# Moving every third injection of the two cross-scan layers to GpSimd, and the product du to VectorE

## The reference

```python
delta = softplus(dts + delta_bias)                    # (192, L)
h = exp(delta * A[d, n]) * h + (delta * u) * B[n, l]  # the recurrence along l
y += h * C[n, l]                                      # summed over n
```

## Time and profile before

| | before |
|---|---|
| median of 3 runs | 3813.66 us (3811.82 to 3817.78) |
| the profiled execution's own time | 3815.76 us |
| its span, first to last instruction | 3813.9 us |
| cross layer 0, first injection to last scan | 1406.3 us |
| cross layer 3, first injection to last scan | 1411.9 us |
| mean granted TensorE clock | 0.779 |

### The profile page before, as it was taken

How to read it: one execution, slowest core, us unless ns; L and a number is a source line. 1 busy time by engine, 2 the same in 40 slices (tenths; PEclk the granted TensorE clock), 3 DMA queues, 4 the chain that set the end, 5 groups by cost and what they waited for, 6 DMA issues and landing times. The chain is left out here.

```text
span 3813.9 us, 26717 instructions
## 1 busy us (share of the span) xinstructions
PE 2849.4 (75%) x6084; PEld 648.1 (17%) x6084; DVE 3266.3 (86%) x2104; ACT 2051.3 (54%) x2278; POOL 2350.1 (62%) x1004
## 2 busy tenths in 40 slices
PE   6778777877887788435667677688778887887887
PEld 2111111111111211111111121111111111111111
DVE  1899999999999998585988924999999999999993
ACT  3465555656565655314555425556565556656562
POOL 1677767777776776003656504677676767776773
PEclk9677787878788877767789777677887778788778
DMA  2555546463655554103443405365546555564742
GB/s 57 136 126 139 138 125 143 119 161 97 160 129 133 124 133 117 28 0 84 117 106 85 99 5 122 99 160 133 129 115 142 135 128 126 132 153 109 157 119 62
DMA packets 140377, 436.95 MB, mean 115 GB/s; under 512 B 33429, under 2 KB 34139, under 8 KB 139915
## 3 DMA queue, kind: packets, MB, share of 16 engines
q1 hardware_dynamic: 140234, 435.53, 47.4%
HBM read 307.50 MB, written 6.82 MB: 82 GB/s over the span
## 5 line engine op out<-in xcount | busy, mean ns | idle before, releaser
L841 POOL TENSOR_TENSOR L_read<-L_state,L_c_rows 128x1024 f32<-128x1024 f32 x768 | 1809.0, 2362 | 757.1 <-DVE L_state L931 467.3
L931 DVE TENSOR_TENSOR_SCAN L_state<-L_decay,L_b_ps 128x1024 f32<-128x1024 f32 x768 | 1756.0, 2286 | 29.4 <-DVE L_b_ps L916 2.1
L651 PE MATMUL L_y_ps<-L_read,L_fold 128*64 128x512 f32 x3072 | 1255.0, 913 | 394.8 <-POOL L_read L841 375.5
L916 DVE TENSOR_TENSOR L_b_ps<-L_du,L_b_ps 128x1024 f32<-128x1024 f32 x768 | 937.5, 1221 | 236.0 <-issue 146.4
L777 ACT ACTIVATE L_decay<-L_delta,L_a_neg 128x1024 f32<-128x1024 f32 x768 | 876.4, 1145 | 406.7 <-DVE L_state L931 405.7
L767 ACT COPY L_b_ps<-L_b_rows 128x1024 f32<-128x1024 f32 x256 | 260.1, 1016 | 340.6 <-DVE L_state L931 220.6
L651 PEld LDWEIGHTS L_y_ps<-L_read,L_fold 128*64 128x64 f32 x3072 | 188.0, 161 | 1356.5 <-POOL L_read L841 1017.6
L1461 POOL TENSOR_TENSOR L_read<-L_state,L_c_rows 128x1024 f32<-128x1024 f32 x96 | 237.3, 2477 | 184.3 <-PE L_y_ps L1257 109.5
L1567 DVE TENSOR_TENSOR_SCAN L_state<-L_decay,L_b_ps 128x1024 f32<-128x1024 f32 x96 | 219.5, 2286 | 3.3
L626 PE MATMUL L_side_ps<-L_dbl,L_w_dt 128*128 128x512 f32 x216 | 182.4, 940 | 50.3 <-DVE L_sq_b L902 26.9
L626 PE MATMUL L_side_ps<-g_cm,L_w_u 96*128 (+1 forms) x216 | 179.7, 921 | 41.7 <-ACT L_u L695 40.0
(11 more groups left out here) (315 smaller groups left out, 2677.3 us busy)
## 6 DMA issues: line engine op xcount, KB each, us to landing
L_c_rows<-L_bc_dram SPq DMA_DIRECT2D x580, 256.0 KB, 4.0
L_b_rows<-L_bc_dram SPq DMA_DIRECT2D x580, 256.0 KB, 4.2
...
```

What stands on the lines that cost most here:

```text
L651: m = nc.tensor.matmul(y_ps[i * BLK:(i + 1) * BLK, c, :], fold[:, :], y_half(t, o, i), start=first, stop=last, skip_group_check=True)
L841: nc.gpsimd.tensor_tensor(read[:, t % READS, :], state[:, t % STATES, :], c_rows[:, g % 2, :], ALU.mult).then_inc(multiplied, 1)
L916: nc.vector.tensor_tensor(to[:, :], du2[:, d * NBLK + c, :], row[:, :], ALU.mult).then_inc(injected, 1)
L931: nc.vector.tensor_tensor_scan(state[:, t % STATES, way], decay[:, t % DECAYS, way], fed[:, way], 0.0, ALU.mult, ALU.add).then_inc(scanned, 1)
```

## The change

It does four things, in the cross-scan layers only. (1) The injection of c = 2 is done by POOL (`inject_c`, L850 in the changed file), from du2 and the SBUF copy of the row B, straight into the state buffer that the scan then reads and overwrites. It stands on POOL ahead of the product with C of c = 0 of its group, and waits for POOL's own last product of the group before, which read that state buffer. `b_rows` gets two buffers for it. (2) The decay of c = 2 goes to a PSUM tile, `work_ps`. This same tile holds the injection of c = 0, so ACT may write the decay of c = 2 only when the scan of c = 0 of that group is done; before, it needed only the scan three tiles back. (3) There is one PSUM tile for the row, `row_ps`; the injection of c = 1 is in place over it. So `copy_b` of the next group still waits for the scan of c = 1, and has only the scan of c = 2 beside it. (4) In the turns du is formed by DVE from the sum in `side_ps`, in two halves of 128 x 512 per block (L929), at tile `at` + 3; ACT's copy of the same half to delta waits for it (`sp_du`). At the heads of the layers POOL still forms du.

```diff
-        b_rows = sb("b_rows", [128, L])
+        b_rows = sb("b_rows", [128, 2, L])
-        b_ps = [ctx.enter_context(nc.psum_tensor(f"{name}_b_ps{i}", [128, L], F32)) for i in range(2)]
+        row_ps = ctx.enter_context(nc.psum_tensor(f"{name}_row_ps", [128, L], F32))
+        work_ps = ctx.enter_context(nc.psum_tensor(f"{name}_work_ps", [128, L], F32))
...
                 sp.wait_ge(b_ready, G + 1)
+                sp.wait_ge(injected_c, G + 1)
...
                 elif kind == "sum":
+                    if not isinstance(turn, Head):
+                        act.wait_ge(sp_du, 2 * (turn.next * NJ + j) + i + 1 - NJ)
                     ins = nc.scalar.copy(delta[:, j, s], side_ps[:, :])
+                    if i == 1:
+                        ins.then_inc(delta_ready, 1)
...
-                    nc.scalar.activation(decay[:, t % DECAYS, :], delta2[:, d * NBLK + c, :], ACT.Exp,
+                    g = t // NBLK
+                    if c == 2:
+
+                        act.wait_ge(scanned, number * NT + t - 1 + SCAN0)
+                    to = work_ps if c == 2 else decay[:, c, :]
+                    nc.scalar.activation(to[:, :], delta2[:, d * NBLK + c, :], ACT.Exp,
...
+            def inject_c(number, g):
+
+                d, last = g // NP, NBLK - 1
+                if g % NP == 0:
+                    pool.wait_ge(du2_in[d * NBLK + last], (number + 1) * PER_BLOCK)
+                pool.wait_ge(b_in[g % 2], (number * (GROUPS // 2) + g // 2 + 1) * 32)
+                pool.wait_ge(multiplied, (number * GROUPS + g) * NBLK + MULT0)
+                nc.gpsimd.tensor_tensor(state[:, last, :], du2[:, d * NBLK + last, :], b_rows[:, g % 2, :],
+                                        ALU.mult).then_inc(injected_c, 1)
...
+                if kind == "sum":
+                    nc.vector.tensor_tensor(du[j][:, s], side_ps[:, :], u[:, j, s], ALU.mult).then_inc(sp_du, 1)
+                    return
...
-                to = row if c == 2 else b_ps[1 - g % 2]
-                if c < 2:
+                to = row_ps if c == 1 else work_ps
+                if c == 0:
                     dve.wait_ge(scanned, T + SCAN0)
...
+                    if c < 2:
+                        by, fed = decay[:, c, :], inject_tile(number, t)
+                    else:
+                        by, fed = work_ps, state[:, c, :]
+                        dve.wait_ge(injected_c, number * GROUPS + g + 1 + READY0)
```

More of the change, by code:

```diff
@@ L449, in cross_scan_layer @@
         c_in = [sem(f"c_in{d}") for d in range(2)]
+        b_in = [sem(f"b_in{d}") for d in range(2)]
         PER_BLOCK = 16 * 2
-        MULT0, SCAN0, SUM0, INJECT0 = NBLK + 1, DECAYS, READS, 1
+        MULT0, SCAN0, SUM0, INJECT0, READY0 = NBLK + 1, DECAYS, READS, 1, 2
         class Turn:
@@ L690, in take @@
                         if j == 0:
-                            act.wait_ge(sp_du, turn.next * NJ)
+                            act.wait_ge(sp_du, turn.next * NJ * 2 - NJ)
                         if j == 2:
@@ L812, in _, with gap @@
         def _(pool):
-            def softplus(turn, kind, j):
+            def gap(turn, j):
                 n = turn.next * NJ + j
-                if kind == "gap":
-                    pool.wait_ge(sp_log, n + 1)
-                    pool.wait_ge(sp_less, n + 1)
-                    l = l_of[j]
-                    nc.gpsimd.tensor_tensor(l[:, :], more[:, :], l[:, :], ALU.subtract).then_inc(sp_gap, 1)
-                else:
-                    wait_side(pool, turn.use(("sum", j), 1))
-                    if not isinstance(turn, Head):
-                        for q in range(2 * j, 2 * j + 2):
-                            pool.wait_ge(du2_in[q], turn.next * PER_BLOCK)
-                    nc.gpsimd.tensor_tensor(du[j], delta[:, j, :], u[:, j, :], ALU.mult).then_inc(sp_du, 1)
+                pool.wait_ge(sp_log, n + 1)
+                pool.wait_ge(sp_less, n + 1)
+                l = l_of[j]
+                nc.gpsimd.tensor_tensor(l[:, :], more[:, :], l[:, :], ALU.subtract).then_inc(sp_gap, 1)
             def add_x(turn):
@@ L844, in turn_of, with form_du @@
                         add_x(turn)
-                    if t in POOL_SOFTPLUS[turn.r]:
-                        softplus(turn, *POOL_SOFTPLUS[turn.r][t])
-            for kind, j in (("gap", 0), ("gap", 1), ("du", 0), ("gap", 2), ("du", 1), ("du", 2)):
-                softplus(Head(), kind, j)
+                    if t in POOL_GAP[turn.r]:
+                        gap(turn, POOL_GAP[turn.r][t])
+            def form_du(j):
+                wait_side(pool, Head().use(("sum", j), 1))
+                nc.gpsimd.tensor_tensor(du[j], delta[:, j, :], u[:, j, :], ALU.mult).then_inc(sp_du, 1)
+            gap(Head(), 0)
+            gap(Head(), 1)
+            form_du(0)
+            gap(Head(), 2)
+            form_du(1)
+            form_du(2)
             over_turns(pool, turn_of)
@@ L892, in finish_side @@
                 done = turn.done_image
+                if kind == "sum" and i == 0:
+                    for q in range(2 * j, 2 * j + 2):
+                        dve.wait_ge(du2_in[q], turn.next * PER_BLOCK)
                 dve.wait_ge(side_ready, use + 1)
+                if kind == "sum":
+                    nc.vector.tensor_tensor(du[j][:, s], side_ps[:, :], u[:, j, s], ALU.mult).then_inc(sp_du, 1)
+                    return
                 if kind == "cent":
```

56 lines of the change are left out of this document (30 added, 26 removed).

## The result

| | median (range), us | over before, 95% interval |
|---|---|---|
| before, in the same call | 3812.74 (3807.25 to 3817.78), 4 runs | |
| changed | 3766.01 (3756.88 to 3783.28), 4 runs | 0.9886 [0.9862, 0.9909] |

The change makes the kernel faster by 1.1%, 47 us. Forecast were 219 us and a range of 3540 to 3665: the sign was right, the size was not, and 171 us are missing.

A forecast was written before the change was run, and what follows sets the result against it. POOL was to replace DVE as the bound; 6 x 165.3 (r = 0), 2 x 161.3 (first turns) and 8 x 160.0 (r = 1) gave 2594.4 us, plus 4.8 of lag, saving 218.9: 3595 us, range 3540 to 3665.

The forecast's parts named there:

- DVE's new path: DVE in the cross layers' turns: group 9.28 us, turn 152.5 us (r = 1 and first turns) or 157.8 (r = 0).
- POOL's own time: POOL in the cross layers' turns, without added waits: group 9.44 us, turn 158.0 us, or 160.3 in r = 0.
- the tie: POOL's injection waits for POOL's own product before it and starts 0.08 us behind it: 2.45 us for this step.
- Rival 1: Port contention between DVE and POOL in the new loop: POOL's instructions at 3.3 us, near 4590 us, slower; chance 4%.
- what is added to POOL's time: Waits on top of POOL's work per turn: in r = 0 2 + 1.5 + 1 us, plus 0.5 for DVE's finish halves.
- PE: Second half of each sum waits for DVE's du and ACT's copy: 0 to 2 us a pair, 1.5 a turn.
- ACT in r = 0: ACT's side operations and halves in tiles 36 to 41, 22 us, mostly beside POOL's gaps: 1 us more.
- The cushion of 2.3 us: POOL's lag allowed before DVE stops at the scan of c = 2; before the change about 6 us.
- Rival 2: The chain of sum, du, copy, sum binds: r = 0 172 us, r = 1 165, total 3687; chance 20% for over 3640.
- du's chain: In the turns: sum half, DVE's du, ACT's copy, next sum half; Rival 2 claimed that it binds.
- ACT's "less" ahead of the gap of block 1: Last softplus of r = 0: POOL waits for ACT's "less", now behind du and its copy, idle 1 to 3 us: 2.
- The sum: All turns of the cross layers added up, 2594.4 us, and 4.8 for lag: 218.9 saved, giving 3595 us.

The follow-up runs named there:

- e8: Changed kernel with ACT taking side halves before the waiting decay of c = 2, and three read buffers instead of two: 3677.59 us.
- e5: Changed kernel with the decay of c = 2 in a third SBUF buffer and without the wait on the scan of c = 0: 4072.66 us.
- e1: Kernel before, with only the wait added: ACT writes the decay of c = 2 once the scan of c = 0 is done: 3852.98 us.
- e6: Changed kernel with ACT taking side halves before the decay of c = 2 that waits, not behind it: 3729.22 us.
- e4: Changed kernel with three read buffers instead of two: 3716.87 us.
- e11: Kernel before with three read buffers, nothing else: 3805.64 us.
- e10: e8 with the two halves of a sum two tiles apart instead of one: 3662.42 us.
- e3: Changed kernel with du formed by POOL in the turns again, as before the change: 3809.91 us.
- e13: Changed kernel with eight fill matmuls on PE at the start of finishing turns and the z halves one tile later: 3760.42 us.
- e15: Changed kernel with the z halves one tile later and no fill matmuls: 3759.62 us.
- e9: e8 with ACT's copy of the row B ahead of the sides and softplus at c = 0: 3674.03 us.
- e12: e10 with the earlier row copy of e9: 3697.96 us.
- e16: e10 with eight fill matmuls on PE at the start of finishing turns and later z halves: 3653.57 us.

## Why the prediction was wrong, point by point

- **DVE's new path and POOL's own time: right.** Group, durations, the 0.08 us of the tie, an order in which POOL is fuller than DVE: all as put down. e8's turns of r = 1 (160.1 us in the mean, forecast 160.0) show the sum for POOL to hold once its waits for PE are gone. The forecast's 161.3 for a first turn doesn't follow from its own terms, which give 158.0 + 2 + 1.5 + 1 = 162.5; that is 2 us in all.
- **Rival 1: right about its mechanism, and rightly kept out.** e5 is what the rival looks like.
- **The failed step** is the part on what is added to POOL's time, its bullets *PE* and *ACT in r = 0*. They counted only the halves of the sums ("Three pairs a turn, 0 to 2 us each, partly in the cushion: 1.5") and held that elsewhere "`copy_b` has 2.25 us beside the scan of c = 2 and needs 1.1". That is true of an ACT that has run ahead, and the change takes its lead once in every group. The edit was read as a wait of the decay, whose own result is in time; the prediction never named what is queued behind the waiting instruction. A half that ACT takes behind the waiting decay can be late, by 2.9 us in the stretch shown, and PE, in order, holds the y of a finished product behind its next half. Where the bullets allowed POOL 1.5 us a turn for PE's lateness, the trace has 177 us, 11 a turn. e1 shows this wait alone to cost 42 us in the kernel before, and e6 gives 37 us back in the changed one by changing only what stands behind it.
- **The cushion of 2.3 us was computed, and used only in part.** It was set against DVE's stop, not against PE's lateness, of which POOL absorbed 6 us before. e4 and its counterpart e11 put a price on it: 49 us in the changed kernel, 5 in the old one. This is what was missing in the turns of r = 1.
- **Rival 2**, with 20%, pointed to late row copies and late halves in du's chain. It gave 165 us for the turns of r = 1 (measured 167.1), but e4 gives their whole excess back with the chain in place, so that is luck. At the end of the turns of r = 0 the chain is there, with 4.2 us a turn of DVE's waits at the halves of du, and 7.4 in e10. The bullet *PE* had 1.5 us a turn for all three pairs. On balance du's move still gains 44 us (e3): 7 us of POOL's work a turn saved against 4 of DVE's was right in sign.
- **ACT's "less" ahead of the gap of block 1**, forecast at 2 us for POOL, is 1.5 in the trace of each finishing turn of layer 0, and 3.7 in its first turn.
- **The sum.** Forecast 3595; the changed kernel 171 us above it; e10 67 above it. So 104 of the 171 us are given back by three edits that touch only the order on ACT, the depth of `read` and the spacing of halves. The 67 us left are the turns of r = 0: 177.5 us in e10 against 165.3, six times 12.2 is 73; the first turns are 10 us above the forecast together and those of r = 1 14 us below it. By place, the excess over POOL's own work is in the first six groups (66.3 us, POOL's work 6 x 9.44 = 56.6) and in the last four (52.4 us, POOL's work 4 x 9.44 + 4.7 = 42.5). In the first, DVE's largest wait is that for the row; in the last, that for PE at the halves of du. Neither the clock at the start (e13 against e15) nor the row's place (e9, e12) accounts for it, and no run takes du's chain away without also loading POOL, so its part stays open.

The fastest versions are e16 and e10, which can't be told from each other: 0.959 to 0.961 of the time before, 2.8 to 3.0% below the changed kernel.
